# Two conditioning pieces moved from an expert layer into the attention before it, and rectified differences in a recurrent attention

## The chip, the cores and the metric

The kernel runs on one core of a Trainium2 chip. The metric is the time of the whole program on the device in microseconds (us). Engines are named as in the profile: PE is TensorE (matmuls; PEld its weight loads), DVE is VectorE, ACT is ScalarE, POOL is GpSimd, SP is SyncE, which here issues the DMAs. Each engine runs its own list of instructions in order and waits on semaphores for the others.

## What is computed

Four blocks run over 1024 tokens of 256 channels (4 rows of 256 tokens). Each block adds an attention and a feed-forward layer to x, and each of the two takes as its input a conditioned x. With the side input f in the place of both k and v, the conditioning is

```python
decay = exp(-exp(w)) * (0.5 + 0.5 * tf)
ek = exp(minimum(f, 30)); ekv = ek * f
nf, df = forward scans of ekv and ek:  a = a * decay + new
nb, db = the same scans backwards
euk = exp(minimum(u + f, 30))
out = sigmoid(x) * (nf + nb - ekv + euk * f) / maximum(df + db - ek + euk, 1e-8) * (0.8 + 0.2 * tf)
```

All but sigmoid(x) depends on f, w and u alone, so the quotient of a layer can be made at any time before that layer. The first attention is causal softmax attention with 32 query heads, 8 key heads and rotary positions; the first feed-forward layer is a mixture of 8 experts (two chosen for each token) with a shared expert. The last attention is a recurrence over the tokens with w = -exp(time_decay) and u = time_first:

```python
mo = maximum(mx, kt + u); e1 = exp(mx - mo); e2 = exp(kt + u - mo)
out = (e1 * num + e2 * vt) / (e1 * den + e2)
ms = maximum(mx + w, kt); e1s = exp(mx + w - ms); e2s = exp(kt - ms)
num, den, mx = e1s * num + e2s * vt, e1s * den + e2s, ms
```

Its output is multiplied by sigmoid(r) and by Wo. The last feed-forward layer is again a mixture of experts.

## The kernel before

x lies transposed in SBUF (`xT`: channels on partitions, in two halves of 128). Eight stages follow one another, each with its own lists for the five engines: `stage_l0_attn` (layer 0, up to about 374 us of the trace), `stage_moe` "L0" (layer 1, up to 523), `stage_l1_attn`, `stage_l1_ffn`, `stage_l2_attn`, `stage_l2_ffn`, `stage_l3_attn` (layer 6, 1078 to 1149) and `stage_moe` "L3" (layer 7, to the end). A stage begins when all engines have left the one before.

**Pieces.** The quotient of a layer is made in `NP` = 8 pieces of 128 channels by 256 tokens, in the course of the layer before it. One piece is, in order: on DVE `piece_scan` step 0 (`uk`, L162) and steps 1 to 4 (four `tensor_tensor_scan`, L167 and L169); on ACT `piece_act` (one Exp, L180); on POOL `piece_sum` steps 0, 1, 2 (L186, L188, L191); on DVE again `piece_quotient` steps 0 (a maximum, L203, which waits for POOL), 1 (`reciprocal`, L206) and 2 (the product into `mod`, L209). There are two sets of buffers, taken in turn (`k`), and three places in `mod` (`l % 3`). `turn_of` numbers the pieces for the semaphores. Where a piece stands among a stage's other work is written out by hand, in each engine's list.

**First attention.** `L0_PAIRS` = 4 pairs of key heads (c = 0 to 3) times `NU` = 16 units (u) make 64 units g = 16c + u; a unit is a pair of heads over one row of tokens. In its list PE does for unit g: `score(g)` (L893), `turn(g - 3)` (transposes, L902 to L904), then one item of `SLOT` (a projection into the single bank `ps_p`, L863 or L869, which needs the bank emptied by ACT's `evac` of the item before) or, at u = 4, 5, 12, 13 of c > 0, a part of the output projection (L876), then `weigh(g - 4)` (L917). DVE does `max_rows(g)` (four masked reductions, L760), `recip(g - 1)` (L766), at the output parts `wo_add` (L773, waits for PE), the rotary steps `rope_sin` (L740) and `rope_add` (L754), and last the steps of the pieces. ACT does `o_evac`, `pt_evac`, `exps(g)` (L656, waits for `max_rows(g)`) and only then `evac` of the item of that unit. POOL does `norm(g)` (L594 and L595, waits for `recip(g)`), piece sums, and `rope_cos` (L588), for which `rope_add` waits. So PE's item of unit u + 1 waits for ACT's `evac` of unit u, which waits behind `exps(u)` for DVE's `max_rows(u)`. Two pieces of layer 1 are made for each pair of heads (one more in the last).

**First expert layer.** `NCH` = 14 chunks of 128 hidden rows. In the first phase PE does `gate_up(ch)` (L1274, 24 matmuls in the three products of a split into high and low parts), which needs DVE's `gu_split(ch)` (L1156) and, for the bank, DVE's product `hid` of the chunk before (L1214, waits for ACT's Silu, L1133). DVE also does `weigh` (L1171) and the pieces of layer 2. ACT's Exp of a piece stands between two Silus, with a table load before and after it. In the second phase PE does `down(ch)` (L1299, 12 matmuls), which needs DVE's `dn_split(ch)` (L1164, L1165), ahead of which stand the last two `weigh`; the steps of pieces 5, 6 and 7 of layer 2 lie between the splits. `unread_products` (L265) are matmuls whose result nobody reads.

**Last attention.** For each half of the channels (ch) DVE makes the running maximum `top` by four scans (L2341) and then five elementwise instructions of 128x1024: `keep1` (L2346), `keep2` (L2348), the maximum for `out2` (L2350), `out1` (L2352) and `out2` (L2353). ACT takes Exp of the four in place (L2313) and later evacuates r (L2304) with a Sigmoid. Then, again for each half, DVE does `grow` (L2357), scans of num and den (L2360, L2363), and the rest up to a `reciprocal` (L2373) and the product into r (L2375), while POOL multiplies (L2287, L2288, and L2290 into r). POOL's first wait is for all of ACT's evacuations (`evac`, 12).

## Time and profile before

| | us |
|---|---|
| median of 3 runs (lowest to highest) | 1309.56 (1307.64 to 1310.96) |
| the profiled execution's own time | 1310.24 |
| its span, from the first to the last instruction | 1308.5 |
| PE busy in the span | 1209.0 (92%) |
| DVE busy | 948.1 (72%) |
| ACT busy | 651.0 (50%) |
| POOL busy | 525.8 (40%) |
| mean granted clock of PE | 0.975 of full speed |

All times in the rows are of the profiled execution, counted from the start of its span. Busy shares are means over eight stages with different limits, so each part of the change is read in its own stage. Waiting time in brackets stands before an instruction, with the one that ended it. PE's matmuls overlap: one ends later than the next begins.

### The profile page before, as it was taken

Reading aid. Unit: us, or ns where it says so; the run is one execution under the profiler, and the core shown is the slowest. Engines: PE = TensorE matmul, PEld = TensorE weight load, DVE = VectorE, ACT = ScalarE, POOL = GpSimd, SP = SyncE. Lnnn points to the kernel's source line nnn. Section 1 sums busy time; section 2 is a strip of 40 time slices with the busy share of each in tenths; the row PEclk is TensorE's granted clock in tenths of the full one; section 3 lists DMA queues with packets and bytes.
Section 4 is the critical chain, followed back from the end, with each engine's and each line's share of the span. In section 5 each row is a group of like instructions: output and inputs, shape, how many; then the busy total and the mean of one; then the engine's idle time right before and its main releaser. Section 6 shows DMA issues by size and latency. Waiting matters only on the chain. (4 is left out here: it accounts for less than half of the span.)

```text
span 1308.5 us, 17043 instructions
## 1 busy us (share of the span) xinstructions
PE 1209.0 (92%) x5978; PEld 848.5 (65%) x5978; DVE 948.1 (72%) x1856; ACT 651.0 (50%) x1503; POOL 525.8 (40%) x423
## 2 busy tenths in 40 slices
PE   6989999999989889999899997999999978599998
PEld 2455556555547767433478875999999953268877
DVE  7967677686857988972634434999999998954355
ACT  3267677767755545544344425444444446053344
POOL 1068676666612221630073330555555530405520
PEclk9999999999999999999889998999999999799999
DMA  2122121221011101400534423111111000011102
GB/s 98 30 80 58 49 57 52 55 49 32 18 34 41 43 22 45 157 1 1 193 110 175 182 74 102 33 34 33 33 33 33 13 3 30 0 50 54 43 28 66
DMA packets 31940, 73.43 MB, mean 56 GB/s; under 512 B 5442, under 2 KB 15171, under 8 KB 29296
## 3 DMA queue, kind: packets, MB, share of 16 engines
q1 hardware_dynamic: 29280, 67.44, 16.8%
q0 software_dynamic: 1536, 3.86, 0.9%
q8 instruction: 48, 0.79, 0.2%
q10 hardware_dynamic: 1040, 1.05, 0.2%
q14 instruction: 36, 0.29, 0.1%
HBM read 55.89 MB, written 6.29 MB: 48 GB/s over the span
## 5 line engine op out<-in xcount | busy, mean ns | idle before, releaser
L186 POOL TENSOR_TENSOR sums<-scans 128x512 f32<-128x512 f32 x56 | 78.7, 1405 | 305.9 <-DVE scans L169 235.0
L594 POOL TENSOR_TENSOR probs<-probs,stats 128x512 f32<-128x512 f32 x64 | 84.0, 1312 | 108.1 <-DVE stats L766 108.0
L656 ACT ACTIVATE probs<-ps_s,stats 128x256 f32<-128x256 f32 (+1 forms) x256 | 104.5, 427 | 39.1 <-DVE stats L760 39.1
L206 DVE RECIPROCAL sums<-sums 128x256 f32<-128x256 f32 x56 | 98.1, 1752 | 1.8
L760 DVE CUSTOM_DVE_ANT_0 ps_s<-ps_s,mask 128x256 f32<-128x256 f32 (+1 forms) x256 | 83.0, 384 | 20.1 <-PE ps_s L893 20.1
L191 POOL TENSOR_TENSOR sums<-sums,terms 128x512 f32<-128x512 f32 x56 | 78.1, 1395 | 4.4
L2123 PE MATMUL K_ps_kvp<-K_wqkv_hi,K_xin_hi 128*128 128x256 f32 x256 | 74.7, 292 | 0.0
L1085 POOL TENSOR_TENSOR L3hid<-L3hid,L3sig 128x1024 f32<-128x1024 f32 x17 | 46.1, 2716 | 70.4 <-DVE L3hid L1214 37.8
L869 PE MATMUL ps_p<-xin,wkvq 128*128 128x512 f32 x144 | 70.1, 610 | 3.8 <-ACT qraw L645 1.8
L2123 PE MATMUL K_ps_kvp<-K_wqkv_lo,K_xin_hi 128*128 128x256 f32 x256 | 72.2, 282 | 0.0
L2123 PE MATMUL K_ps_kvp<-K_wqkv_hi,K_xin_lo 128*128 128x256 f32 x256 | 72.2, 282 | 0.0
L663 ACT ACTIVATE probT<-ps_t 128x768 f32<-128x768 f32 x64 | 52.4, 819 | 33.9 <-PE ps_t L904 33.6
L917 PEld LDWEIGHTS ps_o<-probT,vtok 128*64 128x64 f32 x512 | 31.6, 136 | 53.0 <-issue 22.2
L2005 ACT ACTIVATE K_ks<-K_ps_kvp 128x256 f32<-128x256 f32 x64 | 24.7, 385 | 82.6 <-PE K_ps_kvp L2123 82.6
L893 PE MATMUL ps_s<-kr,qr 64*128 64x256 f32 (+1 forms) x512 | 59.0, 349 | 5.0 <-DVE qr L730 3.4
L1214 DVE TENSOR_TENSOR L3hid<-L3actg,L3ps_u 128x512 f32<-128x512 f32 x34 | 23.3, 687 | 54.4 <-ACT L3actg L1133 54.4
L917 PE MATMUL ps_o<-probT,vtok 128*64 128x256 f32 (+1 forms) x512 | 55.7, 338 | 4.5 <-ACT oT L671 4.5
L893 PEld LDWEIGHTS ps_s<-kr,qr 64*128 64x128 f32 x512 | 44.1, 186 | 21.9 <-issue 10.5
L1835 PE MATMUL E_ps<-E_dT,E_fc 128*128 128x256 f32 x256 | 56.6, 379 | 0.6 <-ACT E_dT L1656 0.6
L169 DVE TENSOR_TENSOR_SCAN scans<-ekv,decay 128x255 f32<-128x255 f32 x64 | 57.0, 890 | 0.0
L1849 PE MATMUL E_ps<-E_fc,E_hid 128*128 128x256 f32 x256 | 56.4, 379 | 0.0
L595 POOL TENSOR_TENSOR probs<-probs,stats 128x256 f32<-128x256 f32 x64 | 56.1, 877 | 0.0
(417 smaller groups left out, 3552.6 us busy)
## 6 DMA issues: line engine op xcount, KB each, us to landing
E_fc<-l_fc_dram SPq DMA_DIRECT2D x16, 1024.0 KB, 7.2
qswap<-qraw SPq DMA_DIRECT2D x60, 128.0 KB, 2.3
ahead<-l_wqkv_dram SPq DMA_DIRECT2D x16, 384.0 KB, 3.3
L3wgu<-L_w_dram SPq DMA_DIRECT2D x17, 256.0 KB, 2.6
L0wgu<-L_w_dram SPq DMA_DIRECT2D x14, 256.0 KB, 2.6
L3wdn<-L_w_dram SPq DMA_DIRECT2D x17, 128.0 KB, 2.0
wkvq<-w_l0a_dram SPq DMA_DIRECT2D x4, 512.0 KB, 4.0
wo<-w_l0a_dram SPq DMA_DIRECT2D x4, 512.0 KB, 3.6
```

What stands on the lines that cost most here:

```text
L169: ins = dve.tensor_tensor_scan(scans[:, k, kind, 1, 0:T - 1][:, ::-1], part(src, i)[:, 1:T][:, ::-1], dec.to_broadcast([P, T - 1]), 0.0, A ...
L186: pstep.mark(pool.tensor_tensor(sums[:, k, :, :], scans[:, k, :, 0, :], scans[:, k, :, 1, :], ALU.add))
L191: pool.tensor_tensor(sums[:, k, :, :], sums[:, k, :, :], terms[:, k, :, :], ALU.add).then_inc(sums_ready, 1)
L206: dstep.mark(dve.reciprocal(den, den))
L594: pool.tensor_tensor(p1, p1, rs[:, 0:2].unsqueeze(2).to_broadcast([P, 2, T]), ALU.mult)
L656: ins = act.activation(dst[:, i % 2, :], src[:, i % 2, :], ACT.Exp, bias=stats[:, g % 4, 4 + i:5 + i], scale=-1.0, accum_out=stats[:, g % ...
L760: ins = dve.tensor_tensor_reduce(out=view, in0=view, in1=m, scale=-1.0, scalar=-NEG, op0=ALU.add, op1=ALU.min, accum_out=stats[:, g % 4, 4 ...
L869: ins = pe.matmul(ps[:, :], w[:, k, :], xin[:, k, h * HALF:(h + 1) * HALF], start=(k == 0), stop=(k == CH - 1))
L893: ins = pe.matmul(view[:, r, :], qr[h, (4 * c + m) % 2, b * T + tile * P:b * T + tile * P + P], kr[h, c % 2, b, 0:n], start=True, stop=True)
L917: ins = pe.matmul(o, vtok[:, c % 2, 2 * b + key, 64 * r:64 * r + 64], probT[:, g % 2, r, 0:256] if key == 0 else probT[:, g % 2, r, 256:38 ...
L1835: ins = pe.matmul(ps[:, h, i * CAP:(i + 1) * CAP], fc1[:, k, c, f:f + P], dT[:, c, e * CAP:(e + 1) * CAP], start=(c == 0), stop=(c == CH - 1))
L2123: ins = pe.matmul(ps_kvp[:, h, a, :], x[:, k, t:t + P], w[:, j // 2, k, P:3 * P], start=(k + m == 0), stop=(k == CH - 1 and m == 2))
```

## The change

It has two parts that share no stage.

1. Pieces 0 and 1 of layer 2 are made in the first attention in place of the first expert layer. `next_piece(p)` now counts on from the eight pieces of layer 1 into layer 2. Pairs c = 1, 2, 3 make three pieces each: 3c - 2, 3c - 1, and a third, 3c, whose scans stand at u = 12 to 15 and whose sums and quotient stand at u = 0, 1, 3, 4 of the next pair; in the last pair the third one's quotient is done in the expert layer, ahead of the router's result. The expert layer makes pieces 2 to 7, all of their scans in its first phase, and only the last quotient in the second.
2. In the last attention DVE makes two differences for each half of the channels: `keep1` = before + decay - k and `out2` = k + first - before. ACT makes of each the two exponents by Relu of the difference and of its negative and takes Exp with scale -1. So six of DVE's ten instructions go and ACT gets eight more. POOL waits for ACT's evacuations only ahead of its product into r.

```diff
             def next_piece(p):
-                return l + 1, HALF_FIRST[p], p % 2
+                return (l + 1, HALF_FIRST[p], p % 2) if p < NP else (l + 2, p - NP, p % 2)
...
                         norm(c * NU + u)
+                        if c > 1 and u == 0:
+                            piece_sum(pool, *next_piece(3 * c - 3), 0)
+                        if c > 1 and u == 1:
+                            piece_sum(pool, *next_piece(3 * c - 3), 1)
+                            piece_sum(pool, *next_piece(3 * c - 3), 2)
                         if u == 3 and c:
-                            piece_sum(pool, *next_piece(2 * c - 1), 0)
+                            piece_sum(pool, *next_piece(3 * c - 2), 0)
...
-                        if c == LAST and u == 13:
-                            piece_act(act, *next_piece(NP - 1))
+                        if c and u == 13:
+                            piece_act(act, *next_piece(3 * c))
...
+                        if c > 1 and u == 3:
+                            piece_quotient(dve, *next_piece(3 * c - 3), 0)
+                            piece_quotient(dve, *next_piece(3 * c - 3), 1)
+                        if c > 1 and u == 4:
+                            piece_quotient(dve, *next_piece(3 * c - 3), 2)
...
+                        if 0 < c < LAST and u in (12, 13, 14, 15):
+                            for step in {12: (0, 1), 13: (2,), 14: (3,), 15: (4,)}[u]:
+                                piece_scan(dve, *next_piece(3 * c), step)
                 recip(ALL - 1)
-                piece_finish(dve, *next_piece(NP - 1))
...
                 gu_split(0)
+                quotient_steps(1, (0, 1, 2))
                 after(dve, "router_done", 1)
...
-                scan_steps(0, (0,))
-
                 for ch in range(NCH):
-                    i = ch // 2
+                    i = ch // 2 + 1
...
-                        if i < NP - 1:
-                            if ch % 2 == 0:
-                                scan_steps(i, ((1, 2), (3, 4))[h])
-                            elif h == 0 and i < NP - 2:
+                        if ch % 2 == 0 and ch:
+                            scan_steps(i, ((1, 2), (3, 4))[h])
+                        elif ch % 2 and h == 0:
+                            if i > 2:
                                 quotient_steps(i - 1, (0,))
+                            if i < NP - 1:
                                 scan_steps(i + 1, (0,))
-                            elif h == 1 and i < NP - 2:
-                                quotient_steps(i - 1, (1, 2))
+                        elif ch % 2 and i > 2:
+                            quotient_steps(i - 1, (1, 2))
...
                     if ch == 2:
-                        quotient_steps(NP - 3, (0, 1, 2))
-                        scan_steps(NP - 1, (0,))
+                        quotient_steps(NP - 1, (0, 1))
                     if ch == 3:
-                        scan_steps(NP - 1, (1, 2))
-                    if ch == 4:
-                        scan_steps(NP - 1, (3, 4))
-                    if ch == 5:
-                        quotient_steps(NP - 2, (0, 1))
-                    if ch == 6:
-                        quotient_steps(NP - 2, (2,))
-                    if ch == 8:
-                        quotient_steps(NP - 1, (0, 1))
-                    if ch == 9:
                         quotient_steps(NP - 1, (2,))
...
-                pool.wait_ge(s["evac"], 12)
...
+                    if ch == 0:
+                        pool.wait_ge(s["evac"], 12)
...
                         act.wait_ge(s["diff_ready"], 2 * ch + j + 1)
+                        diff, other = pair if j == 0 else pair[::-1]
+                        act.activation(other[:, ch, :], diff[:, ch, :], ACT.Relu)
+                        astep.link(act.activation(diff[:, ch, :], diff[:, ch, :], ACT.Relu, scale=-1.0))
                         for x in pair:
-                            ins = act.activation(x[:, ch, :], x[:, ch, :], ACT.Exp)
+                            ins = act.activation(x[:, ch, :], x[:, ch, :], ACT.Exp, scale=-1.0)
...
-                    dve.scalar_tensor_tensor(out=wave(keep1[:, ch, :]), in0=before, scalar=decayed, in1=after,
-                                             op0=ALU.add, op1=ALU.subtract)
-                    dve.tensor_tensor(wave(keep2[:, ch, :]), kc, after, ALU.subtract).then_inc(s["diff_ready"], 1)
...
+                    dve.scalar_tensor_tensor(out=wave(keep1[:, ch, :]), in0=before, scalar=decayed, in1=kc,
+                                             op0=ALU.add, op1=ALU.subtract).then_inc(s["diff_ready"], 1)
+                    dve.scalar_tensor_tensor(out=wave(out2[:, ch, :]), in0=kc, scalar=first, in1=before,
```

Where no line of the diff is shown, the other lists of the first attention and of the expert layer (POOL's and ACT's) get the same renumbering of pieces.

**DVE in the first attention, end of unit 15 of pair 1, where three steps of a quotient stand before the next unit's `max_rows`.** The two ISA rows are one of its four reductions. Before:

```order
L760 ISA ps_s,stats<-ps_s,mask 128x128
L760 ISA stats 128x1
L766 RECIPROCAL stats<-stats 128x4
L203 TENSOR_SCALAR sums<-sums 128x256
L206 RECIPROCAL sums<-sums 128x256
L209 SCALAR_TENSOR_TENSOR mod<-sums,gain 128x256
L760 ISA ps_s,stats<-ps_s,mask 128x256
```

And now (its lines stand five further down in the file):

```order
L765 ISA ps_s,stats<-ps_s,mask 128x128
L765 ISA stats 128x1
L771 RECIPROCAL stats<-stats 128x4
L203 TENSOR_SCALAR sums<-sums 128x256
L206 RECIPROCAL sums<-sums 128x256
L209 SCALAR_TENSOR_TENSOR mod<-sums,gain 128x256
L169 SCALAR_TENSOR_TENSOR scans<-ek,decay 128x255
L765 ISA ps_s,stats<-ps_s,mask 128x256
```

The last backward scan of the third piece now stands ahead of the next pair's first `max_rows`; its other steps stand likewise in units 12, 13 and 14, and two steps of its quotient ahead of unit 3's own scans.

**DVE in the first expert layer, from the last Silu products to the first splits of the second phase.** Before:

```order
L169 SCALAR_TENSOR_TENSOR scans<-ek,decay 128x255
L1214 TENSOR_TENSOR L0hid<-L0actg,L0ps_u 128x512 x2
L1171 TENSOR_TENSOR L0hid<-L0hid,L0sig 128x1024 x3
L1164 TENSOR_TENSOR L0wdn_lo<-L0wdn,L0wdn_hi 128x256
L1165 TENSOR_TENSOR L0xin_lo<-L0hid,L0xin_hi 128x512 x2
```

And now:

```order
L1220 TENSOR_TENSOR L0hid<-L0actg,L0ps_u 128x512
L203 TENSOR_SCALAR sums<-sums 128x256
L1220 TENSOR_TENSOR L0hid<-L0actg,L0ps_u 128x512
L1178 TENSOR_TENSOR L0hid<-L0hid,L0sig 128x1024
L206 RECIPROCAL sums<-sums 128x256
L209 SCALAR_TENSOR_TENSOR mod<-sums,gain 128x256
L1178 TENSOR_TENSOR L0hid<-L0hid,L0sig 128x1024 x2
L1171 TENSOR_TENSOR L0wdn_lo<-L0wdn,L0wdn_hi 128x256
```

The quotient of piece 6, which stood among the splits of the second phase, now stands ahead of the first of them.

**ACT in the last attention, from the evacuation of v to that of r.** Now:

```order
L2301 ACTIVATE V_v<-V_ps 128x512 x4
L2310 ACTIVATE V_keep<-V_keep 128x1024
L2311 ACTIVATE V_keep<-V_keep 128x1024
L2313 ACTIVATE V_keep<-V_keep 128x1024 x2
L2310 ACTIVATE V_out<-V_sig 128x1024
L2311 ACTIVATE V_sig<-V_sig 128x1024
L2313 ACTIVATE V_out<-V_out 128x1024
L2313 ACTIVATE V_sig<-V_sig 128x1024
```

Two Relus (L2310, L2311) have come ahead of each two Exps (L2313), and no table load stands between them; these eight instructions come once for each half of the channels.

## Rows read from the trace of the kernel before

**Rows 1.** Windows: length; busy us of PE, PEld, DVE, ACT, POOL; TensorE clock; DMA.
```profile
146.00:217.00 71.00, 69.29 (x422) 41.57 (x418) 53.39 (x165) 48.30 (x155) 46.52 (x41) 1.00 0.21 49
...
404.00:480.00 76.00, 69.07 (x290) 53.46 (x288) 71.96 (x93) 38.81 (x55) 21.42 (x18) 1.00 0.11 33
...
1078.00:1150.00 72.00, 48.68 (x103) 20.47 (x103) 65.27 (x69) 26.18 (x34) 13.85 (x9) 0.83 0.04 15
```

**Rows 2.** Windows, VectorE's scans alone, in the first attention and expert layer.
```profile
76.00:360.00 284.00, 36.27 (x32) 1.00 0.19 48
404.00:475.00 71.00, 15.13 (x24) 1.00 0.12 34
```

**Rows 3.** Groups by line, VectorE, 76 to 360 us.
```profile
L206 DVE RECIPROCAL sums<-sums 128x256 f32<-128x256 f32 x7 | 12.3, 1753 | 0.2
...
L203 DVE TENSOR_SCALAR sums<-sums 128x256 f32<-128x256 f32 x7 | 7.0, 994 | 8.6 <-POOL sums L191 8.6
...
L209 DVE SCALAR_TENSOR_TENSOR mod<-sums,gain 128x256 f32<-128x256 f32 x6 | 2.8, 473 | 0.1
L162 DVE TENSOR_SCALAR uk<-fside,vecs 128x256 f32<-128x256 f32 x8 | 2.8, 344 | 0.0
```

**Rows 4.** Timeline, TensorE, first attention: start, us, instruction, idle before and releaser.
```profile
205.93 1.98 PE L869 MATMUL ps_p<-xin,wkvq 128*128 128x512 f32 x4 [0.66 <-ACT qraw L645]
...
215.12 2.05 PE L863 MATMUL ps_p<-wkvq,xin 128*128 128x128 f32 x16 [0.50 <-ACT vtok L649]
```

**Rows 5.** Timeline, VectorE, the same turn between two pairs.
```profile
208.13 1.11 DVE L203 TENSOR_SCALAR sums<-sums 128x256 f32<-128x256 f32 x1 [2.22 <-POOL sums L191]
...
211.47 0.42 DVE L760 CUSTOM_DVE_ANT_0 ps_s<-ps_s,mask 128x256 f32<-128x256 f32 x1
...
221.78 1.99 DVE L754 TENSOR_TENSOR qr<-t 128x1024 f32<-128x1024 f32 x1 [1.51 <-issue]
...
231.53 0.69 DVE L773 TENSOR_TENSOR xT<-xT,ps_p 128x512 f32<-128x512 f32 x1 [2.90 <-PE ps_p L876]
```

**Rows 6.** Timeline, GpSimd, the same turn.
```profile
219.33 2.36 POOL L588 TENSOR_TENSOR t<-qraw,rope 128x1024 f32<-128x1024 f32 x1
...
230.28 1.27 POOL L186 TENSOR_TENSOR sums<-scans 128x512 f32<-128x512 f32 x1
```

**Rows 7.** Timeline, TensorE, first expert layer.
```profile
392.56 0.77 PE L1274 MATMUL L0ps_g<-L0xin_hi,L0wgu_hi 128*128 128x512 f32 x1 [3.28 <-DVE L0hid L1214]
...
481.36 0.50 PE L1299 MATMUL L0ps_y<-L0xin_hi,L0wdn_hi 128*128 128x512 f32 x1 [0.89 <-DVE L0xin_lo L1165]
...
520.80 0.39 PE L1299 MATMUL L0ps_y<-L0xin_hi,L0wdn_lo 128*128 128x512 f32 x1
521.03 1.88 PE L265 MATMUL L0ps_g<-fside,ident 128*128 128x512 f32 x4
```

**Rows 8.** Windows, TensorE, four microseconds of the expert layer: busy, granted clock.
```profile
392.00:396.00 4.00, 3.44 (x9) 0.57 0.24 66
```

**Rows 9.** Timelines, ScalarE and VectorE, chunks 4 and 5 of the expert layer.
```profile
419.56 0.60 ACT L1133 ACTIVATE L0actg<-L0ps_g 128x512 f32<-128x512 f32 x1
...
424.45 0.68 DVE L1214 TENSOR_TENSOR L0hid<-L0actg,L0ps_u 128x512 f32<-128x512 f32 x1
```

**Rows 10.** Timelines of the last attention: ScalarE, VectorE, GpSimd.
```profile
1100.61 1.99 ACT L2313 ACTIVATE V_keep<-V_keep 128x1024 f32<-128x1024 f32 x2
...
1108.76 1.04 ACT L2313 ACTIVATE V_sig<-V_sig 128x1024 f32<-128x1024 f32 x1
...
1111.11 2.06 ACT L2304 ACTIVATE V_r<-V_ps 128x512 f32<-128x512 f32 x4
...
1107.68 1.22 DVE L2357 TENSOR_TENSOR V_grow<-V_keep,V_v 128x1024 f32<-128x1024 f32 x1
...
1124.24 1.23 DVE L2375 TENSOR_TENSOR V_r<-V_r,V_sig 128x1024 f32<-128x1024 f32 x1 [0.33 <-POOL V_r L2290]
...
1121.97 2.17 POOL L2290 TENSOR_TENSOR V_r<-V_r,V_num 128x1024 f32<-128x1024 f32 x1
```

More of the change, by code:

```diff
@@ L1087, in _ @@
                 for ch in range(NCH):
[L1088 to L1089 removed]
+                    if more and ch and ch % 2 == 0:
+                        piece_pool(pool, l + 1, ch // 2 + 1, (ch // 2 + 1) % 2)
                     if not more:
@@ L1143, in _ @@
                     dn_split(ch)
-                    if more and ch == 2:
-                        piece_act(act, l + 1, NP - 1, (NP - 1) % 2)
                 if more:
```

48 lines of the change are left out of this document (20 added, 28 removed).

## Prediction

> **What bounds the kernel now.** I read the busy time by stage first [rows 1], then each stage's timeline where an engine starts late. In the first attention (one pair of heads takes 71 us) PE is busy for 69.3 and DVE for 53.4: PE is the bound. In the first phase of the expert layer DVE is busy for 72.0 of 76 us and PE for 69.1: DVE is the bound. In the last attention DVE is busy for 65.3 of 72 us and PE's clock is at 0.83 in the mean: again DVE.
>
> But the attention's mean hides its turns from one pair to the next. There PE stands still for 0.66 and 0.50 us, each time until ACT has emptied the bank of the projection [rows 4]. ACT empties it behind the exponents of the same unit, and these wait for DVE's `max_rows`; the one of unit 0 comes at 211.47 [rows 5], right behind a quotient that had waited 2.22 us for POOL. So at the turn the chain DVE, ACT, PE already has no slack, and a microsecond put on DVE there goes to PE.
>
> **Part 1a, what is put into the attention.** DVE's price of a piece there: four scans 36.27 / 8 = 4.5 us [rows 2], `uk` 0.34, the maximum 0.99, the reciprocal 1.75, the product 0.47 [rows 3], 8.1 in all. A scan costs 1.13 here and 0.63 in the expert layer [rows 2], because DVE and POOL stop each other: the maximum at 208.13 took 1.11 for 256 columns while POOL ran. What is added stands at the turns from pair 1 to 2 and from pair 2 to 3. I follow the first.
>
> (i) Before unit 14's `max_rows` stands one more scan, and `uk` and one scan more stand before unit 13's; these two lie in a wait for PE, but POOL's normalisation of unit 12 and its rotary product for k (2.36, as in [rows 6]) come later by them, and so does `rope_add` on DVE. With the scan of unit 14, unit 15's `max_rows` comes 2.5 to 3 us late. The exponents and the bank's evacuation follow it; more than half of this is slack, since PE had no wait at unit 0 [rows 4]. PE: 1.0. (ii) The fourth scan, 1.3 us, stands ahead of `max_rows` of unit 0, whose slack is gone [rows 4]: PE: 1.2. (iii) In unit 2 `rope_add` had waited 1.51 us for POOL's rotary product [rows 5]; a piece sum of 1.27 [rows 6] now stands ahead of that product, so `max_rows` of unit 3 and the evacuation behind it come 1.3 later; about 0.3 is slack. PE: 1.0. (iv) In unit 3 DVE waits for that piece's total from POOL, then does the maximum and the reciprocal, 2.7 us and more, ahead of its own two scans. `wo_add` of unit 4 had waited 2.90 us for PE [rows 5], which hides most of it; the rest reaches PE's next bank. PE: 1.1.
>
> One turn costs 4.3 us, two 8.6. From below it is nothing: DVE has 17.6 idle us for each pair [rows 1], and 8.1 would fit if they lay right. From above it is the whole work, 16.2. I take 8.6, nearer to the lower middle, since the stalls of [rows 4] show that the turn has no room and the waits of [rows 5] show where room is. The removed quotient at the attention's end lay in a wait for the output projection: 0. The quotient that comes to the head of the expert layer (2.5 us) lies in DVE's wait for the router: 0; without that cover it would be on the path in full.
>
> The Trainium skill (SBUF — State Buffer, Who interferes with whom and the section on its two sides) says that the port pair which DVE and GpSimd share is held by one of them for a whole instruction, and by DVE also for an elementwise operation with two SBUF inputs. The trace agrees, by the 1.11 us for 256 columns. By that rule a piece that met POOL idle would cost DVE 6.1 us in place of 8.1 (scans at 0.63), and by this price the two turns would take 6.5 in place of 8.6.
>
> **Part 1b, what is taken from the expert layer.** First phase: chunks 2 and 3 lose a maximum, a reciprocal and a product, and chunks 0 and 1 the work in DVE's waits. DVE then reaches chunk 4 early and waits for ACT, whose Silu of its second half starts at 419.56 behind two table loads [rows 9] and moves by 0.3 only, the `uk` that no longer stands ahead of chunk 1 [rows 3]. From there DVE needs 0.6 + 0.6 + 1.1 + 1.2 + 0.6 us (the rest of the Silu, the product, `weigh`, two scans, `gu_split`) and reaches its next product at 423.4 in place of 424.45 [rows 9]: -1.0. All later chunks have the same work on DVE as before, so the 1.0 stays and doesn't grow.
>
> Turn to the second phase: the quotient of piece 6 (reciprocal and product, 2.2 us) now stands ahead of the last two `weigh` and the first split, for which PE had waited 0.89 us [rows 7]. +2.2, and PE's wait becomes 3.1 us. A wait of 3.28 us at 392.56 [rows 7] was followed by a granted clock of 0.57 over the next four microseconds [rows 8], the lower of the two levels (1.2 GHz) for most of them, which cost about 1.5. I expect the same here: +1.5.
>
> Second phase: the first to the last matmul take 481.36 to 521.03, 39.7 us, for 13 chunks of 12 matmuls at 0.23 each, 35.4 [rows 7]. The 4.3 between are waits for DVE's splits behind scans and reciprocals of pieces 5 to 7. Only the last piece's quotient is left there, ahead of chunk 3's split, when DVE is ahead: -4.3. Between nothing and -4.3, I take it whole, since ACT too loses the Exp it had waited with. Part 1b: -1.0 + 2.2 + 1.5 - 4.3 = -1.6.
>
> **Part 2, the last attention.** DVE loses six instructions of about 1.2 us (as the one at 1107.68, [rows 10]), 7.3 us, before `grow`. ACT gets eight of about 1.0 us (two Exps took 1.99, [rows 10]), and it can't start before 1100.61, when v is evacuated, as before. Sixteen at 1.0 end at 1116.6; the first four at 1104.7, so `grow` starts 2.9 us earlier than 1107.68, not 7.3. Then POOL's last product needs r. From the last Exp's end, 1109.80, to that of r, 1113.17, ACT took 3.4 us [rows 10]; now r is ready at 1120.0, POOL's product of 2.17 ends at 1122.3, and DVE's product into r starts 1.9 us before its old 1124.24. The rest follows it unchanged: -1.8. Bounds: -2.9 if r doesn't end last (POOL's moved wait lets its first two products go ahead), and +1 if Relu takes longer than Exp by a tenth and the links add to it.
>
> A Relu has no row in this trace; I take Exp's duration, the same engine and shape. The Trainium skill (ScalarE: Activation LUTs, Rules for kernel authors) speaks against the move: it wants `relu` on VectorE, which it calls up to three times as fast in bf16. Here, in fp32, the rows have 1.22 on DVE and 1.0 on ACT. By the page's advice this part would be a loss, say +1 in place of -1.8, and the sum 2.8 us higher. No row of the trace can show the Relu itself.
>
> **The sum.** +8.6 - 1.6 - 1.8 = +5.2 us on the profiled execution's own 1310.24, 1315.4. That execution lies 0.7 above the median of the runs, so for the median 1309.56 + 5.2 = 1314.8. A measurement of this kernel can tell about 0.3%, 3.9 us, from no change: up to 1305.6 is faster, from 1313.5 on slower.
>
> **Rivals.**
> A. The attention takes the pieces in its idle DVE time, and the change is a gain. Its mechanism: the lag at the turns is made good inside the 2.90 us and 2.22 us waits of DVE [rows 5] before it reaches a bank. Then the attention costs at most 1, and the time is 1309.56 + 1 - 1.6 - 1.8 = 1307.2, or 1305.7 if the clock also stays up, since the wait of 3.1 is a little shorter than that of 3.28. It decides for faster when the lag of unit 0's `max_rows` stays below about 1 us. For it: DVE idles for a quarter of each pair. Against it: the stalls at just these places [rows 4]. 0.22, of it 0.09 faster.
> B. DVE becomes the bound of whole pairs, each added microsecond is paid: 1309.56 + 16.2 - 3.4 = 1322.4. Against it: six units in the middle of each pair have nothing added. 0.08, slower.
> C. The relocation works as in the forecast, but ACT's sixteen instructions take all that DVE saves: last attention +1, 1317.6. 0.05, slower.
> D. The change does not do what it says (a table load between Relu and Exp, at two loads for each pair of functions). The order of ACT's instructions has none, and I give it no chance of its own.
> By the skill's page on activation a fifth would be part 2 as a loss; that is C's time, and C's chance stands for it.
>
> **Chances.** My forecast, 1311 to 1318 (attention +5 to +11.5 by the price of a met or unmet POOL, clock kept or not), has 0.65: 0.52 slower by over 0.3%, 0.13 within. With A's 0.09 faster and 0.13 within, B's and C's 0.13 slower: faster 0.09, within 0.26, slower 0.65. The likeliest is 1314.8. The range must leave out no more than 0.2: B above and the lower half of A go out, 1307.5 to 1319.
>
> **What would show it.** In the changed profile: in the first attention PE's waits for ACT in units 0, 1, 4 and 7 of pairs 2 and 3 grow to some 1 to 1.5 us, and the stage ends 8 to 9 us later; pair 1 up to unit 13 is as before. In the expert layer PE waits about 3 us before the first L1299 of the split chunks, with a lower clock behind it, and none before the later ones; the stage takes 1.6 us less. In the last attention there is no new table load, `grow` starts 2.9 us earlier in the stage, and DVE waits about 2 us for POOL ahead of its product into r. I am wrong if the attention ends within 2 us of its old end, or if r's evacuation isn't what POOL waits for.

## The result, and the profile after

The changed kernel takes 1314.69 us (median of 17 runs, 1309.76 to 1316.79), the kernel before 1308.32 us (17 runs beside them, 1305.71 to 1310.96). The ratio is 1.004, with a 95% interval of 1.003 to 1.005: slower, by 6.4 us between the medians and by 5.2 between the means. The forecast was 1314.8, with a range of 1307.5 to 1319. The number is met, and the question is whether its terms are. The profiled execution of the changed kernel took 1316.29 us, its span is 1314.5, 6.0 more than before.

The difference of the two spans by stage, from the first instruction of each stage on TensorE in the two timelines (for the expert layers that is the first of the eight `unread_products` that they begin with):

| stage | before, us | after, us | difference |
|---|---|---|---|
| start to the first expert layer | 374.85 | 382.52 | +7.7 |
| first expert layer | 148.6 | 145.7 | -3.0 |
| next stages, from the first product into `R_ps` to the first into `K_ps_kvp` | 281.3 | 283.7 | +2.4 |
| from there to the last attention's first product | 281.4 | 281.3 | -0.1 |
| last attention, from there to the last expert layer | 63.8 | 61.8 | -2.0 |
| last expert layer | 158.5 | 159.5 | +1.0 |

The third, the fourth and the last line belong to code that the change doesn't touch. They come up again at the end.

**The first attention.** I measure it by the starts of `max_rows` on VectorE, one for each unit (the units are counted through all pairs, so unit 16 is unit 0 of pair 1). Up to unit 16 the code is the same. From 16 to 63 it is 219.74 us before and 227.16 after, +7.4. A pair is the same stretch from its middle to the next one's middle, so one turn is the distance from unit 24 to 40: 76.52 before, 80.38 after, +3.86; the next, 40 to 56, gives 76.52 and 80.39. These are the rows at the first turn. VectorE's timeline after:

```profile
207.49 0.40 DVE L765 CUSTOM_DVE_ANT_0 ps_s<-ps_s,mask 128x256 f32<-128x256 f32 x1
...
210.03 1.11 DVE L203 TENSOR_SCALAR sums<-sums 128x256 f32<-128x256 f32 x1 [1.18 <-POOL sums L191]
...
213.97 0.41 DVE L765 CUSTOM_DVE_ANT_0 ps_s<-ps_s,mask 128x256 f32<-128x256 f32 x1
...
225.48 2.00 DVE L759 TENSOR_TENSOR qr<-t 128x1024 f32<-128x1024 f32 x1 [2.71 <-issue]
...
230.01 1.12 DVE L203 TENSOR_SCALAR sums<-sums 128x256 f32<-128x256 f32 x1 [1.23 <-POOL sums L191]
...
233.95 0.41 DVE L765 CUSTOM_DVE_ANT_0 ps_s<-ps_s,mask 128x256 f32<-128x256 f32 x1
...
240.99 0.69 DVE L778 TENSOR_TENSOR xT<-xT,ps_p 128x512 f32<-128x512 f32 x1 [2.33 <-PE ps_p L888]
```

GpSimd's timeline after:

```profile
221.82 1.26 POOL L186 TENSOR_TENSOR sums<-scans 128x512 f32<-128x512 f32 x1
223.04 2.34 POOL L588 TENSOR_TENSOR t<-qraw,rope 128x1024 f32<-128x1024 f32 x1
```

TensorE's timeline after, with the same place of the next turn (287.83 and 297.99), and five windows of a microsecond behind the first wait (columns as in [rows 1]):

```profile
207.46 3.15 PE L881 MATMUL ps_p<-xin,wkvq 128*128 128x512 f32 x4 [1.93 <-ACT qraw L650]
...
231.32 3.67 PE L888 MATMUL ps_p<-oT,wo 128*128 128x512 f32 x8 [0.83 <-ACT qraw L650]
...
287.83 1.98 PE L881 MATMUL ps_p<-xin,wkvq 128*128 128x512 f32 x4 [1.93 <-ACT qraw L650]
...
297.99 2.05 PE L875 MATMUL ps_p<-wkvq,xin 128*128 128x128 f32 x16 [1.46 <-ACT vtok L654]
```
```profile
207.00:208.00 1.00, 0.54 (x2) 0.30 (x3) 1.00 (x4) 1.00 (x3) 1.00 (x3) 1.00 0.00 0
208.00:209.00 1.00, 1.00 (x3) 0.49 (x2) 0.86 (x7) 0.61 (x2) 0.92 (x2) 0.57 0.00 0
209.00:210.00 1.00, 1.00 (x2) 0.03 (x1) 0.00 (x0) 1.00 (x5) 1.00 (x2) 0.50 0.00 0
210.00:211.00 1.00, 1.00 (x3) 0.30 (x4) 0.96 (x1) 0.94 (x5) 1.00 (x3) 0.50 0.00 0
211.00:212.00 1.00, 1.00 (x10) 0.62 (x8) 0.96 (x2) 0.48 (x2) 0.62 (x1) 0.73 0.09 16
```

Unit 15's `max_rows` at 207.49 is 2.72 us later within the turn than before (35.34 against 32.62 us behind unit 24's). TensorE's wait of 0.66 [rows 4] has become 1.93, and its four matmuls took 3.15 us where they took 1.98. The granted clock, third from the right in the windows, says why: it is at 0.50, the lower level (1.2 GHz), for some 3.5 us behind that wait. Before, this place had none. But the low clock costs the turn nothing. The next turn has the same wait of 1.93 and keeps the full clock, its four matmuls take 1.98 us again, and it is as long (80.39 for 80.38): TensorE then waits 1.46 us at 297.99, a wait that the first turn doesn't have. GpSimd's sum at 221.82 stands ahead of the rotary product, as predicted, and unit 3's `max_rows` is 1.22 us later for it (9.49 for 8.27 us behind unit 33's).

**The first expert layer.** TensorE's timeline after, against [rows 7]:

```profile
398.73 0.47 PE L1270 MATMUL L0ps_g<-L0xin_hi,L0wgu_hi 128*128 128x512 f32 x1 [0.28 <-DVE L0hid L1220]
...
487.51 0.50 PE L1295 MATMUL L0ps_y<-L0xin_hi,L0wdn_hi 128*128 128x512 f32 x1 [3.13 <-DVE L0xin_lo L1172]
...
488.55 0.63 PE L1295 MATMUL L0ps_y<-L0xin_hi,L0wdn_hi 128*128 128x512 f32 x1
...
520.12 0.50 PE L1295 MATMUL L0ps_y<-L0xin_hi,L0wdn_hi 128*128 128x512 f32 x1 [0.78 <-DVE L0xin_lo L1172]
...
525.47 0.39 PE L1295 MATMUL L0ps_y<-L0xin_hi,L0wdn_lo 128*128 128x512 f32 x1
```

The wait of 3.13 us is the predicted one, and eight matmuls behind it start 0.43 us apart and not 0.23: 1.6 us of low clock, also as predicted. Of the waits in the second phase (1.51, 1.54 and 0.20 us before) 0.78 is left.

**The last attention.** ScalarE, VectorE and GpSimd after, against [rows 10]:

```profile
1107.67 1.05 ACT L2310 ACTIVATE V_keep<-V_keep 128x1024 f32<-128x1024 f32 x1
...
1111.73 1.23 DVE L2351 TENSOR_TENSOR V_grow<-V_keep,V_v 128x1024 f32<-128x1024 f32 x1 [4.34 <-ACT V_keep L2313]
...
1124.80 2.06 ACT L2301 ACTIVATE V_r<-V_ps 128x512 f32<-128x512 f32 x4
1127.01 2.17 POOL L2287 TENSOR_TENSOR V_r<-V_r,V_num 128x1024 f32<-128x1024 f32 x1 [1.11 <-ACT V_r L2301]
1129.28 1.23 DVE L2369 TENSOR_TENSOR V_r<-V_r,V_sig 128x1024 f32<-128x1024 f32 x1 [1.30 <-POOL V_r L2287]
```

The stage begins 7.1 us later (TensorE's products of `V_mixed` begin at 1093.2, before at 1086.2). So `grow` is 3.0 us earlier in the stage than 1107.68, r is there at 1126.86, 1119.8 by the old clock, and the product into r is 2.0 us earlier. GpSimd waits for r, and VectorE for GpSimd. A Relu took 1.05 us, as long as an Exp.

### The profile page after: what moved, and what is told of

It is laid out like the page before. It is cut to its first block and busy times, and to the rows that moved or that the text cites. A ratio compares the mean times of both kernels' runs of the same rounds, so it can differ in the third digit from the quotient of the medians.

```text
span 1314.5 us, 17042 instructions
## 1 busy us (share of the span) xinstructions
PE 1213.4 (92%) x5978; PEld 853.1 (65%) x5978; DVE 945.4 (72%) x1850; ACT 654.6 (50%) x1508; POOL 527.5 (40%) x423
## 3 DMA queue, kind: packets, MB, share of 16 engines
q0 software_dynamic: 1536, 3.86, 0.9%
q10 hardware_dynamic: 1040, 1.05, 0.2%
## 5 line engine op out<-in xcount | busy, mean ns | idle before, releaser
L169 DVE TENSOR_TENSOR_SCAN scans<-ekv,decay 128x255 f32<-128x255 f32 x64 | 61.4, 959 | 0.0
L905 PEld LDWEIGHTS ps_s<-kr,qr 64*128 64x128 f32 x512 | 45.0, 190 | 22.2 <-issue 11.1
```

The source lines that it names most:

```text
L169: ins = dve.tensor_tensor_scan(scans[:, k, kind, 1, 0:T - 1][:, ::-1], part(src, i)[:, 1:T][:, ::-1], dec.to_broadcast([P, T - 1]), 0.0, A ...
L905: ins = pe.matmul(view[:, r, :], qr[h, (4 * c + m) % 2, b * T + tile * P:b * T + tile * P + P], kr[h, c % 2, b, 0:n], start=True, stop=True)
```

## The experiments

The kernels in the order of the text: `p1_alone`, `p2_alone`, `quot_later`, `spread10`, `spread10_quot`, `r_between`, `spread8`, `sum_late`, `quot_unit4`, `scans_in_15`. Ratios are to the kernel before, run beside them.

### One part at a time

`p1_alone` is the changed kernel with the last attention of before.

> The moved pieces alone: the last attention is that of the kernel before. Theory (the two parts are independent, and the last attention earned what stands between the ends of its products in the two traces, 2.0 us): attention 7 to 8.5 us longer than before, first expert layer 2.5 to 3.5 us shorter, last attention as before, so the time is 6 to 9 us above the kernel before, about 2 us above the changed kernel. Rival (the two parts are not additive: the later last attention changes nothing, its gain is an effect of the clock's phase): same time as the changed kernel, 5 to 7 us above the kernel before.

Measured: 1314.37 us (8 runs), ratio 1.0047, interval 1.0031 to 1.0063. Attention from unit 16 to 63: 227.13 us, the changed kernel's to 0.03. Expert layer 145.3. Last attention 63.8, as before.

`p2_alone` is the kernel before with the last attention of the change.

> The rectified differences alone, on the kernel before. Theory: 1.5 to 2.5 us below the kernel before; from the last product of V_mixed to the first transpose of V_ps TensorE waits 16.6 us where it waited 18.7; the second difference goes to ScalarE, VectorE is 2.9 us earlier at V_grow, V_r is evacuated after the Exps, GpSimd waits about 1 us for it and VectorE about 1.3 us for GpSimd. Rival (GpSimd's wait or the four more ScalarE passes eat the gain): no difference to the kernel before, within 1 us.

Measured: 1306.17 us (11 runs), ratio 0.9984, interval 0.9973 to 0.9994. Last attention 61.8. The row of the waits that belongs to it, first of before, then of this kernel:

```profile
PE V_ps L265 <- DVE V_r L2375: 18.7, 1, 18.7
```
```profile
PE V_ps L265 <- DVE V_r L2373: 16.6, 1, 16.6
```

What follows: in both traces these two stages add up, 7.4 us in the attention and -2.0 in the last attention, whatever the other part is. By the medians, `p1_alone` is as slow as the whole change, where the theory wanted it 2 us slower. This reading is not decided: 8 runs of a kernel whose runs lie 8 us apart (1310.87 to 1319.24) don't resolve 2 us. Part 2 on its own is faster by its interval.

### The expert layer's quotient

`quot_later` moves one quotient in the changed kernel:

```diff
-                            if i > 2:
+                            if 2 < i < NP - 1:
                                 quotient_steps(i - 1, (0,))
...
-                        elif ch % 2 and i > 2:
+                        elif ch % 2 and 2 < i < NP - 1:
                             quotient_steps(i - 1, (1, 2))
...
                     dn_split(ch)
+                    if ch == 1:
+                        quotient_steps(NP - 2, (0, 1))
                     if ch == 2:
-                        quotient_steps(NP - 1, (0, 1))
+                        quotient_steps(NP - 2, (2,))
                     if ch == 3:
+                        quotient_steps(NP - 1, (0, 1))
+                    if ch == 4:
                         quotient_steps(NP - 1, (2,))
```

> The changed kernel, with the quotient of piece 6 moved from the last chunk's products to behind the first split of the down weights (piece 7's one split later). Theory (the 3.13 us wait before the first split down product is that quotient's 2.4 us ahead of the last two weighings and the first split, and the low clock for some 3 us behind the wait follows from it): the wait falls to 0.7 to 1.0 us, no low clock behind it; the two quotients then stand between the splits, where waits of together 1.5 to 3 us (0.8 now) come back; the expert layer is 1 to 3 us shorter than in the changed kernel. Rival (the quotient's time is only moved; what is won at the wait is lost between the splits): no gain, within 0.7 us.

Measured: 1308.0 us (12 runs), ratio 1.0001, interval 0.9988 to 1.0013, so 6.7 us below the changed kernel. The expert layer took 141.7 us for 145.7. TensorE's timeline, the first and the second split chunk:

```profile
484.41 0.50 PE L1299 MATMUL L0ps_y<-L0xin_hi,L0wdn_hi 128*128 128x512 f32 x1 [0.90 <-DVE L0xin_lo L1172]
...
487.88 0.50 PE L1299 MATMUL L0ps_y<-L0xin_hi,L0wdn_hi 128*128 128x512 f32 x1 [0.45 <-DVE L0xin_lo L1172]
```

The wait is 0.90, no low clock follows it, and of the expected 1.5 to 3 us between the splits only 0.45 came. The profiled executions differ by 4.0 in this stage, more than the 1 to 3 expected: the quotient cost 2.2 us as a wait and 1.6 as a clock, and it costs 0.4 where VectorE runs ahead of the splits. By the means, `quot_later` is 4.8 us below the changed kernel; the rest of the 6.7 between the medians is not explained.

The 1.6 us of clock are no fixed part of that price. Six of the kernels here have the changed kernel's expert layer and its wait of 3.1 us. In five of them the low clock follows; in `quot_unit4` (next heading) it doesn't, by its first split product and the window over it, with the clock at 1.00:

```profile
485.70 0.50 PE L1292 MATMUL L0ps_y<-L0xin_hi,L0wdn_hi 128*128 128x512 f32 x1 [3.14 <-DVE L0xin_lo L1169]
```
```profile
485.00:489.00 4.00, 3.30 (x14) 2.74 (x15) 3.97 (x8) 0.14 (x1) 0.00 (x0) 1.00 0.14 41
```

### One edit at the turn

Three kernels with edits at the turn, each with a profile and a single time; the attention is read by the starts of `max_rows`. `sum_late` writes the piece sums of units 0 and 1 behind `rope_cos`:

> The changed kernel with one edit at the turn: GpSimd's sums of the third piece (units 0 and 1 of pairs 2 and 3) stand behind the rotation's product rope_cos instead of ahead of it. Measured by the starts of max_rows in the traces. Theory (step (iii) of the prediction: the sum ahead of rope_cos makes unit 3 late by 1.0): from unit 33's max_rows to unit 35's 8.3 to 8.6 us (before 8.27, changed 9.49), from unit 24 to unit 40 79.2 to 79.6 (before 76.52, changed 80.38); units 24 to 31 stay at 35.3. Rival (the sum only takes the GpSimd time somewhere else and the turn stays as long): 24 to 40 stays within 0.3 of 80.38.

`quot_unit4` is `sum_late` with VectorE's quotient a unit later:

```diff
-                        if c > 1 and u == 3:
-                            piece_quotient(dve, *next_piece(3 * c - 3), 0)
-                            piece_quotient(dve, *next_piece(3 * c - 3), 1)
                         if c > 1 and u == 4:
-                            piece_quotient(dve, *next_piece(3 * c - 3), 2)
+                            piece_finish(dve, *next_piece(3 * c - 3))
```

> sum_late, and VectorE's quotient of the third piece stands behind unit 4's max_rows instead of unit 3's. Times between starts of max_rows. sum_late left 24 to 40 at 80.36: unit 35's max_rows came 1.0 earlier and VectorE lost it again ahead of unit 36's, where its quotient waited 2.23 us for GpSimd's sum (1.23 in the changed kernel). Theory (that wait is what closes the turn): with the quotient a unit later there is no such wait, unit 36's max_rows comes at least 2 us earlier, and 24 to 40 is 78.5 to 79.6. Rival (the 2.9 us of the quotient and its wait are only handed to the next unit, where TensorE's products for the rotation wait instead): 24 to 40 stays within 0.4 of 80.36.

`scans_in_15` puts the third piece's scans in one place:

```diff
-                        if 0 < c < LAST and u in (12, 13, 14, 15):
-                            for step in {12: (0, 1), 13: (2,), 14: (3,), 15: (4,)}[u]:
+                        if 0 < c < LAST and u == 15:
+                            for step in range(5):
```

> The changed kernel with all five scan steps of the third piece behind unit 15's max_rows (they stood in units 12 to 15), ahead of unit 0's of the next pair. Times between starts of max_rows. Theory (steps (i) and (ii) of the prediction: what the scans cost is what they hold up): 24 to 31 falls from 35.34 to about 32.6, as before, and the 1.9 us wait for qraw near 207 and the low clock behind it are gone; 31 to 32 rises from 6.48 to 8.5 to 10; on 24 to 40 the sum is the same within 1 us (79.4 to 81.4). Rival (behind unit 15 they are hidden, since TensorE has the items of units 14 and 15 and the pair's v products to do there): 24 to 40 falls to 78.5 or less.

Single times: 1313.46, 1309.01 and 1313.07 us. Measured, us between the starts of two units' `max_rows`:

| units | before | changed | sum_late | quot_unit4 | scans_in_15 |
|---|---|---|---|---|---|
| 24 to 31 | 32.62 | 35.34 | 35.33 | 35.34 | 32.62 |
| 31 to 32 | 6.96 | 6.48 | 6.48 | 6.49 | 9.55 |
| 33 to 35 | 8.27 | 9.49 | 8.51 | 8.51 | 9.50 |
| 35 to 40 | 24.72 | 25.14 | 26.11 | 25.07 | 25.12 |
| 24 to 40 | 76.52 | 80.38 | 80.36 | 79.34 | 80.72 |

`sum_late` split the theory. Unit 3 (35 by the table) came 1.0 us earlier, as step (iii) said, and nothing was won: 24 to 40 stayed, which is the rival's reading. The timelines of VectorE and GpSimd in `sum_late` tell where it went:

```profile
221.65 2.35 POOL L588 TENSOR_TENSOR t<-qraw,rope 128x1024 f32<-128x1024 f32 x1
...
229.85 1.12 DVE L203 TENSOR_SCALAR sums<-sums 128x256 f32<-128x256 f32 x1 [2.23 <-POOL sums L191]
...
233.79 0.41 DVE L765 CUSTOM_DVE_ANT_0 ps_s<-ps_s,mask 128x256 f32<-128x256 f32 x1
```

VectorE reaches the quotient a microsecond sooner and waits a microsecond longer for the same sum (2.23 for 1.23), because GpSimd has the same work before it in either order. Unit 36 starts at 233.79 for 233.95. So steps (iii) and (iv) are no sum: they are one chain that closes at the quotient. `quot_unit4` takes the quotient off that place, and now the microsecond comes out: unit 36's `max_rows` is 3.3 us behind unit 35's, for 7.6 in `sum_late`, and 24 to 40 falls by 1.02. The later quotient without `sum_late`'s edit was not run, so what it would bring alone is open. `scans_in_15` shows the same of steps (i) and (ii). Unit 31 comes as in the kernel before, 2.72 us earlier than in the changed kernel, and unit 32 then takes 3.07 longer than there. From 24 to 32 the turn is 42.17 us, for 41.82 in the changed kernel and 39.58 before. TensorE's wait of 1.93 near 207 is gone, and another one stands at unit 33:

```profile
216.90 2.69 PE L875 MATMUL ps_p<-wkvq,xin 128*128 128x128 f32 x16 [2.40 <-ACT vtok L654]
```

Low clock follows this one in the first turn and not in the second (2.41 us there), and again both turns are as long, 80.72 us. At neither place of the turn are the scans hidden.

### The same pieces in other units

`spread10` keeps all ten pieces in the attention and places every step by a table: for each piece the unit of the `uk`, of the four scans, of the Exp, of GpSimd's first and other sums and of the quotient's two parts, and for the sums whether they stand behind the rotary products. Four of its rows:

```diff
+            PLACES = ((4, 8, 8, 10, 11, 5, 11, 13, 15, 15, 0, 0),
+                      (16, 17, 19, 19, 19, 16, 18, 20, 23, 23, 0, 1),
...
+                      (24, 24, 25, 27, 27, 24, 30, 30, 35, 35, 1, 1),
+                      (31, 32, 32, 35, 36, 34, 36, 36, 40, 40, 1, 1),
```

> The changed kernel with the same ten pieces in the first attention, but their steps stand in other units of the pairs (a table of units for each piece's scans, exponential, sums and quotient), mostly in units whose number is 3 of 4 and away from the units 12 to 15 and 0 to 2 of the next pair; nothing else is changed, and the ninth piece's quotient stays in the expert layer. Theory (the moved piece costs because of where its steps stand, ahead of a max_rows or a rotation that TensorE waits for, and VectorE has room elsewhere): the attention ends at least 6 us earlier than in the changed kernel, at or ahead of its end before, with the waits for qraw at the pairs' turns gone; the time is 5 to 15 us below the changed kernel and 1 to 10 below the kernel before. Rival (a third piece in a pair costs some 4 us wherever it stands, because VectorE and GpSimd are short of time over the whole pair): the attention ends within 2 us of that of the changed kernel.

Measured: 1300.44 us (6 runs), ratio 0.9937, interval 0.9923 to 0.9951. Units 16 to 63 took 215.40 us, 11.8 below the changed kernel and 4.3 below the kernel before, with two pieces more than that one. VectorE's timeline at the turn in `spread10`, units 32 and 33:

```profile
205.71 0.43 DVE L787 CUSTOM_DVE_ANT_0 ps_s<-ps_s,mask 128x256 f32<-128x256 f32 x1 [2.15 <-PE ps_s L904]
...
209.95 0.43 DVE L787 CUSTOM_DVE_ANT_0 ps_s<-ps_s,mask 128x256 f32<-128x256 f32 x1 [0.73 <-PE ps_s L904]
```

This is the reading to learn: the `max_rows` of the turn waits 2.15 us for TensorE. In the kernel before [rows 5] and in the changed one the same instruction starts right behind VectorE's other work, with no idle time ahead of it. VectorE is ahead of TensorE again: TensorE's waits from unit 16 to 63 add up to 3.2 us here (those above 0.15 us), 6.2 in the kernel before and 11.1 in the changed one. A piece costs the attention some 4 us if its steps stand at the turn, and far less elsewhere; rival B's idea of a price that is paid anywhere falls. The gain isn't even: 24 to 40 took 74.20 us, 40 to 56 took 77.84, 1.3 more than before. Which entries of the table do it was not tried one by one.

`spread8` asks what the move itself is worth: the kernel before with part 2, its own eight pieces placed by such a table.

> The kernel before with the rectified differences, and its own eight pieces of the first attention spread in the same manner (its expert layer as before: no piece is moved from one stage to the other). This tells what the move is worth once the steps stand well. Theory (with good places a piece in the attention costs nothing, so the move earns what the expert layer is shorter by): attention within 1 us of spread10's (units 16 to 63 in 215 to 216.5 us), expert layer 148 to 149 us, time 1300 to 1302.5, so no more than 2 above spread10 and 3 to 6 above spread10_quot. Rival (two more pieces still cost in the attention): this one's attention is shorter than spread10's by 2 us or more.

Measured: 1302.88 us (6 runs, 1297.27 to 1304.06), ratio 0.9947, interval 0.9926 to 0.9968. Units 16 to 63 took 214.34 us, 1.1 less than in `spread10`, and the expert layer 147.2. So two more pieces cost 1.1 us in the attention, not nothing and not the rival's 2. That holds for these two tables only: they differ in most of their rows, and neither is known to be the best. The old eight pieces, moved to other units, gain 5.4 us by themselves (219.74 to 214.34), so the 11.8 of `spread10` are not the price of the moved pieces alone. The expert layer and the time came out a little off what was expected (148 to 149 and at most 1302.5).

### The best kernels

`spread10_quot` joins `spread10` and `quot_later`.

> The two mends together: the ten pieces of the first attention spread as in spread10, and the quotient of piece 6 behind the first split of the down weights as in quot_later. Theory (they are in different stages and add up): attention as in spread10 (unit 16's first max_rows to unit 63's 215.4 us), the first expert layer some 4 us shorter than in spread10, time 1295 to 1298. Rival (the clock's low stretches fall elsewhere and take the second gain back): 1299 to 1301, as spread10.

Measured: 1297.77 us (4 runs), ratio 0.9913, interval 0.9893 to 0.9933. The expert layer took 143.7 us, 3.4 less than in `spread10` (147.1); its first split product waits 0.89.

`r_between` moves r's evacuation in the last attention:

```diff
                         ins.then_inc(s["exp_ready"], 1)
-                for g in range(8, 12):
-                    evac(g)
+                    for g in range(8, 12) if ch == 0 else ():
+                        evac(g)
```

> spread10_quot, with the evacuation of r in the last attention between the Exps of the first and of the second half instead of behind both. Theory (what GpSimd waits for ahead of its product into V_r is that evacuation, and VectorE then waits for GpSimd): the waits of 1.1 and 1.3 us there are gone, V_r starts right behind the reciprocal, TensorE waits 1.2 to 1.4 us less (15.3 for 16.6), at the price of two more table loads on ScalarE of 1.28 us each that nothing waits for; time 1.0 to 1.4 below spread10_quot. Rival (the second half is late instead: its Exps end some 3.5 us later and VectorE waits for them ahead of its second V_grow or the product behind the scans): no difference or up to 2 us slower.

Measured: 1295.01 us (4 runs, 1293.99 to 1295.49), ratio 0.9895, interval 0.9875 to 0.9915: the fastest kernel of this study, 13.6 us below the kernel before beside it and 2.8 below `spread10_quot`. The last attention took 60.7 us for 61.8. ScalarE, GpSimd and VectorE there:

```profile
1095.97 2.06 ACT L2304 ACTIVATE V_r<-V_ps 128x512 f32<-128x512 f32 x4
...
1099.94 1.28 ACT L2316 ACT_TABLE_LOAD   x1
...
1105.01 2.17 POOL L2290 TENSOR_TENSOR V_r<-V_r,V_num 128x1024 f32<-128x1024 f32 x1
...
1107.29 1.23 DVE L2372 TENSOR_TENSOR V_r<-V_r,V_sig 128x1024 f32<-128x1024 f32 x1 [0.28 <-POOL V_r L2290]
1108.43 1.22 DVE L2354 TENSOR_TENSOR V_grow<-V_keep,V_v 128x1024 f32<-128x1024 f32 x1
```

GpSimd's product no longer waits for ScalarE, VectorE waits 0.28 for 1.30, and the second `grow` has no wait in spite of the later Exps. So r's evacuation is what GpSimd had waited for. The stage gives 1.0 of the 2.8 us between the medians; the rest is not explained.

## Why the prediction was right, and where it was not

**The number** (1314.8 for 1314.69) is right, and so is the side. Its three terms, +8.6, -1.6 and -1.8, sum to 5.2. By what the change itself does in the traces they are +7.4, about 0 and -2.0, which is 5.4. That errors of 1.2 and 1.6 us nearly cancel is luck. The 5.4 fit the 5.2 between the means; the 6.4 between the medians, and the match to 0.1 us with them, are within the scatter of the runs.

**Part 1a** is the mechanism as predicted, at 3.86 a turn for 4.3. (i) and (ii), 2.2 together: from unit 24 to 32 the turn is 2.24 longer. Unit 15's `max_rows` came 2.72 late, within "2.5 to 3 us". TensorE's waits, in the second turn where the clock stays up, are 1.93 and 1.46 us for 0.67 and 0.52 before: 1.3 and 0.9 more, for the 1.0 and 1.2 of the forecast. In the first turn a low clock that I had not predicted here takes the place of the second wait and adds nothing; the starts of `max_rows` in the two turns agree within 0.03 us. `scans_in_15` shows that the two steps are nearly one cost. (iii), 1.0: 1.22 at its place. (iv), 1.1: 0.42, and the step that failed is that I added it to (iii). The signs that I named, four waits of 1 to 1.5 us, came as three, the third of 0.83 us before unit 4's output projection. The quotient waits for a sum that GpSimd ends at the same time either way (`sum_late`). Pair 1 up to unit 13 is as before, as predicted. A pair takes 76.5 us, not the 71 of the window in [rows 1], and VectorE idles for 20.1 us of it, not 17.6, which changes no term. The lower bound, nothing, holds for this placement; with a better one even less is possible (`spread10`), since the old placement had losses of its own.

**The rule of the Trainium skill** (SBUF — State Buffer, Who interferes with whom) gave 6.5 for the two turns against my 8.6, with 7.4 measured between them: no run tells the two prices apart, since what counted was neither 8.1 nor 6.1 us of VectorE but what stood behind them. The exclusive hold is seen again in the changed kernel: the maximum over 256 columns took 1.11 and 1.12 us at the turn beside GpSimd, and 0.28 us at 706.64, where GpSimd is idle.

**Part 1b** was -1.6 and is about 0. The -1.0 of the first phase measured -0.8 (chunk 7, with its wait of 1.42 us, comes 32.0 us behind the first product of `L0sig` where it came at 32.8). The +2.2 measured 2.24 (3.13 for 0.89), the +1.5 of the clock 1.6. The term that was mis-sized is -4.3: from the first to the last matmul the second phase took 39.44 us before and 37.96 after, of which 1.6 is the low clock, so it gave 3.1. A wait of 0.78 stayed, and 0.5 of the 4.3 were no waits but a slip in my sum: 13 times 12 times 0.23 is 35.9, not 35.4. The stage as a whole was 3.0 us shorter all the same, by two stretches of low clock that lay elsewhere: at its start (the first eight transposes took 3.67 us for 5.37), and in chunk 1, which ran at 1.2 GHz behind the wait of 3.28 before and not after. Neither is the change's: `spread8` has the old expert layer with 3.67 us at the start, and `p2_alone` has it with a wait of 0.82 ahead of a chunk 1 at full clock. Two kernels have their low clock at the same place of this layer, 16 us behind its start, and nowhere else: `spread8` with the old layer took 147.2 us, `quot_unit4` with the changed one 145.3. Their difference of 1.9 is 0.9 won in the first phase, 2.2 lost ahead of the first split and 3.2 won behind it; the clock of 1.6 behind the wait, where it comes, leaves 0.3.

**Part 2** was -1.8 and is -2.0. Each step is at its place: `grow` 3.0 earlier for 2.9, r ready at 1119.8 by the old clock for 1120.0, the product into r 2.0 earlier for 1.9, no new table load. I had VectorE waiting 2 us for GpSimd; it was 1.30. `r_between` shows that r's evacuation is the releaser. On Relu, the Trainium skill (ScalarE: Activation LUTs, Rules for kernel authors) advises VectorE, and I had put a loss of 1 us beside that. At 1.05 us for 1024 fp32 columns on ScalarE, against 1.22 to 1.29 for the two-input VectorE operations that went, the move gained 2.0. No run has a Relu on VectorE, so which engine is the faster for a Relu alone isn't shown here.

**The rivals.** A had the idle VectorE time of each pair for it, and the placement is what it got wrong: the room is there, as `spread10` shows, but not in the waits at the turn that A named. `sum_late` shows what one of them is worth: the microsecond won ahead of it only made it longer. B is out by `spread10` too. C would have had the last attention at +1; it is -2.0.

## What to carry to other kernels

- Before you put work beside a bound engine, look at the instruction that the bound engine waits for, not at the idle share of the one you load. Here VectorE idled a quarter of every pair, and 8.1 us of its work cost 3.9 at one place and about 0.5 at others (1.1 for two pieces, between two tables made by hand). Idle time ahead of the instruction that feeds TensorE ([2.15 <-PE]) says that there is slack at that place; that a step put there is free was not tried by itself.
- Late steps that meet in one wait are not to be added up. Take one of them away alone: if the end stays, another holds it. Here the first edit paid nothing, and the two together 1.0 us.
- A wait ahead of dense matmuls costs its length and, in five of six traces here, some clock. A quotient of 2.2 us cost 3.8 in front of the first split (2.2 in the sixth trace) and 0.4 a few chunks on.
- Look behind a low clock before you count it: at the attention's turn it took the place of a wait and cost nothing, behind the first split it cost 1.6 us.

## What the runs showed of the hardware

The low stretches of TensorE's clock lie at different places of code that is the same, from one profiled execution to another. The same wait is not always followed by one: 1.93 us in the attention (yes at the first turn, no at the second) and 3.1 us in the expert layer (yes in five kernels, no in `quot_unit4`). The part from the first product of `E_dT` and `E_fc` to the first into `K_ps_kvp` is the same in all kernels, and took 138.9 to 142.0 us in the twelve profiled executions. Before and after differ by 2.0 there. TensorE has long waits in it, at the same distance from its start; windows of 12 us, before and, 5 us later as the stage is, after:

```profile
788.00:800.00 12.00, 7.00 (x20) 3.78 (x21) 7.18 (x15) 6.83 (x13) 0.61 (x2) 0.57 0.25 83
800.00:812.00 12.00, 11.25 (x62) 8.61 (x61) 5.13 (x6) 6.40 (x13) 2.52 (x2) 1.00 0.45 131
```
```profile
793.00:805.00 12.00, 7.23 (x20) 3.93 (x21) 7.72 (x15) 7.42 (x14) 0.60 (x2) 0.59 0.29 97
805.00:817.00 12.00, 11.25 (x49) 7.41 (x48) 4.57 (x5) 4.77 (x10) 2.52 (x2) 0.84 0.26 78
```

After, the low level (0.84 in the mean of the second window) still holds when the ten `unread_products` of the next stage begin, and they pay for it, 6.6 us for 4.0 up to the first product into `K_ps_q`: 49 matmuls lie in the window for 62. In the last expert layer the place decides the price. TensorE comes to chunk 1 some 16 us behind the layer's start and waits for VectorE there. In three kernels (before, `p1_alone`, `spread8`) the low stretch begins 7 us behind the start and slows chunk 0; TensorE's wait ahead of chunk 1 is 1.5 us, and the layer took 158.5 to 158.7 us. In eight others nothing slows chunk 0, that wait is 3.0 us, the low stretch stands over chunk 1 and isn't covered by any wait, and the layer took 159.5 to 160.4. (`r_between`, with a longer stretch over chunk 0, took 159.2.) Windows of the layer and the first product of chunk 1, before and after:

```profile
1150.00:1164.00 14.00, 14.00 (x64) 10.66 (x64) 10.03 (x29) 9.35 (x11) 0.00 (x0) 0.88 0.28 79
1164.00:1178.00 14.00, 12.45 (x64) 10.36 (x63) 6.46 (x8) 5.37 (x8) 2.68 (x2) 1.00 0.14 39
```
```profile
1165.82 0.47 PE L1274 MATMUL L3ps_g<-L3xin_hi,L3wgu_hi 128*128 128x512 f32 x1 [1.55 <-DVE L3hid L1214]
```
```profile
1155.00:1169.00 14.00, 12.73 (x64) 9.50 (x64) 10.12 (x29) 10.40 (x13) 0.00 (x0) 1.00 0.28 78
1169.00:1183.00 14.00, 12.23 (x55) 10.24 (x56) 4.84 (x8) 4.04 (x6) 1.12 (x1) 0.88 0.14 39
```
```profile
1170.77 0.76 PE L1270 MATMUL L3ps_g<-L3xin_hi,L3wgu_hi 128*128 128x512 f32 x1 [3.02 <-DVE L3hid L1220]
```

So a gain of 2.0 us in the last attention can be given back next door, up to 1.9 us of it, without a change there. Whether part 2 itself brings this about is not decided: both kernels with the old last attention have the cheap place, and eight of the ten with the new one the dear one. The 17 runs of the changed kernel (1309.76 to 1316.79) go the same way: the six fastest had a mean granted clock of 0.973 to 0.974, the others 0.968 to 0.973. So a stage's length is the better measure of an edit than one execution's end, and differences of 1 to 2 us between medians of 4 to 12 runs are left open above.
